# Second attention of a vision tower: the place counts move ahead of the output product, and three scatter DMAs move ahead of the next root

## The reference

```python
h = tok(x) ; h = h + attn0(layernorm(h)) ; h = h + moe0(layernorm(h))
h = h + attn1(layernorm(h))        # the second attention
h = h + moe1(layernorm(h))         # 8 experts, top 2 of each token
...
# attn1, B=8 batches of 1024 tokens, 128 channels:
attn = softmax(einsum('bisc,bjsc->bisj', qb, kb) * scale)
out = einsum('bisj,bjsc->bisc', attn, vb) @ W_proj + b_proj
# moe1:
top_vals, top_idx = top_k(flat @ Wr, 2) ; top_w = softmax(top_vals)
out = sum over the chosen e of top_w * (gelu(flat @ W1[e] + b1[e]) @ W2[e] + b2[e])
```

## Time and profile before

| what | value |
|---|---|
| median of 3 runs | 1414.62 us (1414.47 to 1420.9) |
| the profiled execution | 1414.32 us, of which the span is 1412.5 us |
| busy PE, DVE, ACT, POOL over the span | 84%, 66%, 70%, 40% |
| mean granted clock of PE | 0.917 of full speed |
| roots of the second attention, b = 0 to 7 | 880.2 to 1046.3 us |
| first expert rows read after the stage | 1097.1 us |

### The profile page before, as it was taken

How to read it: one execution, slowest core, us unless ns; L and a number is a source line. 1 busy time by engine, 2 the same in 40 slices (tenths; PEclk the granted TensorE clock), 3 DMA queues, 4 the chain that set the end, 5 groups by cost and what they waited for, 6 DMA issues and landing times. The chain is left out here.

```text
span 1412.5 us, 26983 instructions
## 1 busy us (share of the span) xinstructions
PE 1181.6 (84%) x9386; PEld 794.1 (56%) x9386; DVE 934.5 (66%) x2612; ACT 994.4 (70%) x1348; POOL 561.7 (40%) x546
## 2 busy tenths in 40 slices
PE   3599999999999999979989987787861799999940
PEld 2344444444444444447768865676761688888830
DVE  4366868686868686669878873777651466666625
ACT  0498888888888888769768975445420799999930
POOL 3413333343434343211110010377776177677660
PEclk9799999999999999889999997788865899999975
DMA  3664737373737374232113100011116377777619
GB/s 86 119 177 99 178 98 180 96 182 94 187 89 187 86 191 104 76 131 77 60 60 120 61 0 1 17 46 46 47 46 232 119 238 240 236 248 246 231 28 354
DMA packets 93164, 180.58 MB, mean 128 GB/s; under 512 B 15597, under 2 KB 64200, under 8 KB 84960
## 3 DMA queue, kind: packets, MB, share of 16 engines
q1 hardware_dynamic: 72832, 129.18, 32.3%
q0 software_dynamic: 17344, 42.68, 9.3%
q10 hardware_dynamic: 2848, 6.95, 1.7%
HBM read 116.96 MB, written 63.12 MB: 127 GB/s over the span
## 5 line engine op out<-in xcount | busy, mean ns | idle before, releaser
L741 ACT ACTIVATE a_probs<-a_psS 128x1024 f32<-128x1024 f32 x512 | 483.1, 1034 | 83.1 <-PE a_psS L826 51.8
L838 PE MATMUL a_psO<-a_probs,a_v 128*32 128x256 f32 x4096 | 277.5, 389 | 17.7 <-DVE a_o_t L1015 17.4
L1252 DVE TENSOR_TENSOR f_g_lo<-f_g,f_g_hi 128x512 fp32r<-128x512 f32 x284 | 195.2, 689 | 116.7 <-ACT f_g L1159 115.4
L2043 POOL DMA_INDIRECT result<-f_out,f_idx x156 | 180.6, 1158 | 101.4 <-issue 57.6
L838 PEld LDWEIGHTS a_psO<-a_probs,a_v 128*32 128x32 f32 x4096 | 107.5, 110 | 151.6 <-issue 85.1
L1630 POOL DMA_INDIRECT queue<-all_row,all_idx x128 | 125.8, 983 | 38.6 <-issue 37.6
L826 PE MATMUL a_psS<-ag_qs,ag_ks 50*128 50x512 f32 x512 | 95.8, 450 | 12.8 <-DMA ag_qs<-a_gparts 5.9
L826 PE MATMUL a_psS<-a_qs,a_ks 50*128 50x512 f32 x512 | 96.4, 452 | 8.8 <-issue 4.6
L402 POOL TENSOR_TENSOR ag_rs_f<-ag_veps_f,all_half 128x4 f32<-128x4 f32 x32 | 33.9, 1058 | 124.7 <-DVE ag_veps_f L99 124.7
L1422 POOL TENSOR_TENSOR ah_rs<-ah_veps,all_half 128x4 f32<-128x4 f32 x16 | 18.5, 1154 | 154.3 <-DVE ah_veps L1435 154.2
L826 PEld LDWEIGHTS a_psS<-ag_qs,ag_ks 50*128 50x128 f32 x512 | 39.3, 188 | 59.6 <-ACT a_probs L741 30.2
(11 more groups left out here) (368 smaller groups left out, 2879.7 us busy)
## 6 DMA issues: line engine op xcount, KB each, us to landing
all_w<-experts SPq DMA_DIRECT2D x19, 1026.5 KB, 5.4
experts<-a_split POOLq DMA_DIRECT2D x32, 512.0 KB, 5.0
ag_qs<-experts SPq DMA_DIRECT2D x14, 1026.5 KB, 5.5
ag_ks<-experts SPq DMA_DIRECT2D x14, 1026.5 KB, 5.2
f_rows<-queue SPq DMA_DIRECT2D x39, 260.0 KB
f_w<-experts SPq DMA_DIRECT2D x8, 1026.5 KB, 5.4
qparts<-a_parts SPq DMA_DIRECT2D x16, 512.0 KB, 4.3
kparts<-a_parts SPq DMA_DIRECT2D x14, 512.0 KB, 3.2
```

Of the source, the lines that this page charges most:

```text
L741: nc.scalar.activation(probs[u % NPR][:, :], psS[score_buffer(u)][:, :, :].rearrange("p a n -> p (a n)"), ACT.Exp).then_inc(exp_done, 1)
L838: last = nc.tensor.matmul(psO[32 * g:32 * g + 32, a * HALF:(a + 1) * HALF], v[par][:, 2 * hp + p, kt, :], probs[u % NPR][:, cols:cols + HA ...
L1252: nc.vector.tensor_tensor(g_lo[i][:, n, :], g[:, n, :], g_hi[i][:, n, :].bitcast(F32), ALU.subtract).then_inc(lo_done, 1)
L2043: pool.indirect_dma_start(result, bass.IndirectOffsetOnAxis(ap=idx[i][:, j:j + 1], axis=0), out[i][:, j, :], None, bounds_check=2 * B * S ...
```

## The change

On PE, `positions(b - 1)` is issued ahead of `output(b)`. On DVE, `route(b - 1)` is issued ahead of `add(b)`. On POOL, `send` takes a range of its 16 DMAs; in iteration b the first three of `send(b - 1)` are issued ahead of `root(b)` and the other 13 behind it. No instruction is added or taken away apart from semaphore waits: a split `send` tests its two semaphores twice.

```diff
+    EARLY = 3
...
-            def send(n):
+            def send(n, lo=0, hi=K * T):
                 pool.wait_ge(slot_done, n + 1)
                 pool.wait_ge(row_done, n + 1)
-                for k in range(K):
-                    for t in range(T):
-                        pool.indirect_dma_start(queue, bass.IndirectOffsetOnAxis(ap=idx[n % NROW][:, k, t:t + 1], axis=0),
-                                                row[n % NROW][:, k, t, :], None).then_inc(sent[n % NROW], 16)
+                for i in range(lo, hi):
+                    k, t = divmod(i, T)
+                    pool.indirect_dma_start(queue, bass.IndirectOffsetOnAxis(ap=idx[n % NROW][:, k, t:t + 1], axis=0),
+                                            row[n % NROW][:, k, t, :], None).then_inc(sent[n % NROW], 16)
...
             for b in range(B):
+                if b:
+                    send(b - 1, 0, EARLY)
                 root(b)
                 if b:
-                    send(b - 1)
+                    send(b - 1, EARLY)
             send(B - 1)
...
                     project(b + 1, 0)
-                output(b)
                 if b:
                     positions(b - 1)
+                output(b)
...
                     apply_x(b + 2)
+                if b:
+                    route(b - 1)
                 add(b)
                 moments_z(b)
-                if b:
-                    route(b - 1)
                 apply_z(b)
```

## The result

The changed kernel took 1441.3 us (median of 4 runs, 1432.32 to 1447.12), the kernel before, run beside it, 1417.76 us (4 runs, 1414.47 to 1429.35). The ratio is 1.0151, with a 95% interval of 1.0112 to 1.0189: slower, as forecast, by twice the forecast amount and outside the range. The profiled execution took 1437.98 us, 23.7 us more than that of before.

The account below looks back on a forecast made before the run. It took a dependency circle through PE, DVE and POOL, period 23.78 us, as the bound. 11.6 + 1.4 - 2.3 = +10.7 us on 1414.32 gave 1425.0, predicted as 1425.3 us for the median; range 1417 to 1434 us.

Parts of the forecast that it names:

- The chain and the direction: PE, b = 1 to 6: `positions` ahead of `output` delay the chain 1.93 us each, 11.6 us, nothing coming back; slower 0.81.
- Route ahead of add at price 0: DVE, b = 1 to 6: `route`'s 1.56 us fills time in which DVE waits for `output`, costing 0.
- The estimate of half a microsecond: Root without `route` beside it: 0.5 us won per iteration by the skill's page; the forecast used the rows' 0.03 us instead.
- DMAs ahead of the root: POOL: three DMAs, 3.8 us, delay no root with 1.5 us to spare, and save 2.3 us behind the last root.
- I take 1.93, since they would follow `project` at the upper clock: PE, b = 1 to 6: `positions` ahead of `output` cost 1.93 us each at the upper clock; bounds 0 and 3.85 us.
- rival A: PE: the clock falls inside the later output product, 2.6 us each; three of seven 1433 us, all seven 1443; chance 0.22.
- the last iteration: PE, b = 7: `positions` ahead of `output` cost 1.4 us at the upper clock; 3.4 us at the lower.
- B: PE: the low-clock stretch over `logits` and `attend` shifts and gives part of the delay back, 1418.5 us; chance 0.14.
- Rival C: PE: the low-clock stretch leaves the chain, POOL bounds at 22.40 us an iteration, 1404 us, faster; chance 0.04.

Follow-up runs that it names:

- e1: The kernel before with only PE's order changed, `positions` ahead of `output`; ratio 1.0184 against the kernel before.
- e2: The changed kernel without the DMAs ahead of the root, keeping PE's and DVE's new order; ratio 1.0186 against the kernel before.
- e5_wide_delay: The kernel before with 8 dummy products of 128 columns ahead of `output`, `positions` still behind it; ratio 1.0078 against the kernel before.
- e8_narrow_delay: The kernel before with 9 dummy products of the widths of `positions` ahead of `output`, real `positions` still behind it; ratio 1.0223 against the kernel before.

## Why the prediction was half right

*The chain and the direction: right.* `output` starts later by the length of `positions`, 2.0 us measured against 1.93, nothing behind it gives this back, and the short iterations are 1.9 to 2.2 us longer than before. The order on PE alone gives the loss (e1).

*Route ahead of add at price 0: right* (e2). The root beside which no `route` runs now took 1.67 us, as with it before. The estimate of half a microsecond worked out by the Trainium skill (SBUF — State Buffer, Who interferes with whom) did not appear.

*DMAs ahead of the root: right in place, nearly in size.* 2.7 us won at the end against 2.3; they delayed no root, each of which waited 1.5 to 3.8 us for the variance behind them.

*The step that failed* is the clock of the product behind `positions`. The 1.93 us themselves held: `positions` took 2.0 us, at the upper level, in all six iterations. But "I take 1.93, since they would follow `project` at the upper clock" puts nothing into the sum for the product behind them, as if it stayed at the upper level too. In three of the six iterations the clock fell inside it, and it took 5.24 to 5.26 us instead of 3.31. I had priced this fall as rival A and given it 0.22, because before the change the upper level held over `positions`. That argument overlooked where they stood then, behind the wide matmuls of the product's second half and ahead of the wide `project`. The runs showed (`e5_wide_delay` against `e8_narrow_delay`) that the narrow work lowers the clock, not the delay. The bias matmuls of one row begin the product behind the wide work too, where the clock held, so alone they do not do it.

*By the terms, from the first root to the last:* 189.60 us against 166.11 us, +23.5 us where I had 13.0. Three iterations of the short kind cost 1.9 to 2.2 us each, three of the long kind 4.6 to 4.9 us, and the last 2.9 us (I had 1.4, the whole product being at the lower level there). The long iterations thus make some 8 us of the missing 10.5 us, the last iteration 1.5 us. Of the 8 us the product took 5.8 (1.93 us each) and `project` 1.8: it took 2.4 us instead of 1.8, being at the lower level for longer. A's price was 2.6 us for each affected product, worked out for both halves at the lower level; the same 2.6 us came out as product and `project` together, and that is luck. Before the first root the profiled execution was 2.3 us later than before, in stages that the change does not touch, and at the end 2.7 us were won.

*The waits of rivals A and B.* The wait ahead of `turn_z` grew, as A said it would: from 0.5 us to 2.51 us in the long iterations and 1.4 us in two of the three short ones. B's argument that the wait of 3.31 us ahead of `logits` stays as it is held in the short iterations alone; in the long ones it was 2.44 us.

*Rival C, turned round.* The low stretch was worth what C said, POOL's own pace, but it had to be taken away by other work; the change itself made it longer.

Open is why every second iteration is hit. The traces show this much: in the three long iterations the clock had fallen in the wait of 2.51 us ahead of `turn_z` and rose 0.4 us ahead of `positions`; in the three short ones it fell in the wait ahead of `logits` and rose 1.1 us ahead of them. No run fixed these points.

## What to carry to other kernels

Work that stands behind a chain on its engine was free here; put ahead of the chain it cost its full length, though `route` and the first DMAs then started earlier. Before moving short, narrow matmuls in front of a critical product, ask what they do to the clock of what follows, and read the granted clock of that stretch: in this kernel it fell with PE busy throughout. Where PE waits on a chain that PE bounds, wide dummy matmuls in the wait can be worth more than a new order: here 0.7%, until POOL became the bound.

## What the runs showed that I had not expected

The clock fell while PE was busy without a pause: 3.41 of 3.41 us between a rise at 925.59 and a fall at 929.00, of which 2.0 us were `positions` and some 0.65 us bias matmuls of one row. And 13 dummy products ahead of `logits` suffice to take most of the low stretch away (0.9933), while seven among the router's products, where the matmuls are narrow, make the kernel slower (1.011).
